# Second attention of a two-layer block: where half of V's product stands in TensorE's order, and where its copies stand in ScalarE's

## The reference

```
h = _ln(x, ln1_g, ln1_b) + shift                  # 256 features
qkv = (h @ Wqkv.T).reshape(b, n, 3, H, HD)        # H = 16, HD = 64
q = _ln(qkv[:, :, 0].transpose(0, 2, 1, 3), qn_g, qn_b)
k = _ln(qkv[:, :, 1].transpose(0, 2, 1, 3), kn_g, kn_b)
v = qkv[:, :, 2].transpose(0, 2, 1, 3)
scores = einsum('bhnd,bhmd->bhnm', q, k) / sqrt(HD)
attn = softmax(scores, axis=-1)
o = einsum('bhnm,bhmd->bhnd', attn, v)
x = x + o.transpose(0, 2, 1, 3).reshape(b, n, H * HD) @ Wout.T
gate = softmax(x.reshape(-1, d) @ Wgate.T, axis=-1)
```

## Time and profile before

| what | value |
|---|---|
| time before, median of 3 runs | 2434.58 us (2432.95 to 2436.35) |
| the profiled execution's own time | 2434.36 us |
| its span, first to last instruction | 2432.5 us |
| mean granted TensorE clock over the span | 0.970 |
| second attention, by the first and the last product that L1431 makes | 831.2 to 1929.9 us |
| TensorE busy over the span | 2318.0 us |
| VectorE, ScalarE, GpSimd busy | 1909.5, 1548.8, 1030.9 us |

### The profile page before, as it was taken

One profiled execution on the slowest core, in us unless ns is written; L12 is line 12 of the kernel. 1 busy time (PEld: TensorE's weight loads), 2 busy tenths in 40 slices (PEclk: granted clock), 3 DMA queues, 4 the chain that ended last, 5 costly groups with the idle time before them and its releaser, 6 DMA issues. The chain is left out here.

```text
span 2432.5 us, 67113 instructions
## 1 busy us (share of the span) xinstructions
PE 2318.0 (95%) x24912; PEld 2059.8 (85%) x24912; DVE 1909.5 (78%) x3776; ACT 1548.8 (64%) x2983; POOL 1030.9 (42%) x939
## 2 busy tenths in 40 slices
PE   7999999999999899999999999999999818999997
PEld 6888888899999788888888888888888717999996
DVE  8999999667667788888888888888888777666663
ACT  6999998766666456565656565656565554556653
POOL 5888888200000234343434343434343203445544
PEclk9999999999999899999999999999999856999998
DMA  4111110101001000000000000000000022334423
GB/s 146 43 41 41 43 39 25 53 25 32 28 26 33 27 17 15 16 14 17 13 17 13 17 13 17 13 17 13 17 13 17 15 61 71 91 95 87 97 52 35
DMA packets 78720, 89.21 MB, mean 37 GB/s; under 512 B 18480, under 2 KB 72496, under 8 KB 76080
## 3 DMA queue, kind: packets, MB, share of 16 engines
q1 hardware_dynamic: 66352, 71.10, 9.4%
q0 software_dynamic: 12288, 17.05, 4.3%
HBM read 62.42 MB, written 25.69 MB: 36 GB/s over the span
## 5 line engine op out<-in xcount | busy, mean ns | idle before, releaser
L1286 POOL TENSOR_TENSOR a_rq<-a_vq,minus_half 128x8 f32<-128x8 f32 x256 | 417.7, 1641 | 97.5 <-DVE a_vq L1310 97.5
L1230 ACT ACTIVATE a_sq<-a_bqk 128x512 f32<-128x512 f32 x256 | 152.9, 597 | 351.3 <-PE a_bqk L130 348.7
L1281 POOL TENSOR_TENSOR a_rstd<-a_veps,minus_half 128x1 f32<-128x1 f32 x63 | 34.8, 552 | 580.5 <-DVE a_veps L1357 580.5
L128 PE MATMUL a_bqk<-wqk_hi,a_h_lo 128*128 128x512 f32 x512 | 207.7, 406 | 3.5 <-DVE a_h_lo L1326 3.5
L130 PE MATMUL a_bqk<-wqk_hi,a_h_hi 128*128 128x512 f32 x512 | 201.2, 393 | 0.0
L129 PE MATMUL a_bqk<-wqk_lo,a_h_hi 128*128 128x512 f32 x512 | 201.0, 393 | 0.0
L1302 DVE TENSOR_TENSOR a_qk<-a_bqk,a_rq 128x512 f32<-128x512 f32 x256 | 175.9, 687 | 29.6 <-POOL a_rq L1286 29.5
L1956 ACT ACTIVATE e_u<-e_bu,e_b 128x512 f32<-128x512 f32 x128 | 88.3, 690 | 150.1 <-PE e_bu L130 147.7
L1215 ACT COPY a_vs<-a_ba 64x512 f32<-64x512 f32 x256 | 148.8, 581 | 53.5 <-PE a_ba L130 48.8
L2081 DVE TENSOR_TENSOR e_u_lo<-e_u,e_u_hi 128x512 fp32r<-128x512 f32 x128 | 88.4, 691 | 120.4 <-ACT e_u_hi L1961 120.3
L1294 DVE TENSOR_REDUCE a_ss<-a_sq 128x8 f32<-128x512 f32 x256 | 173.9, 679 | 2.6 <-ACT a_sq L1230 1.0
(11 more groups left out here) (334 smaller groups left out, 8036.6 us busy)
## 6 DMA issues: line engine op xcount, KB each, us to landing
a_qk<-gates_of_rows SPq DMA_DIRECT2D x32, 256.0 KB, 4.3
tokens<-a_xs SPq DMA_DIRECT2D x64, 128.0 KB, 1.7
out<-a_xs SPq DMA_DIRECT2D x64, 128.0 KB, 1.7
e_w<-in_fc1s SPq DMA_DIRECT2D x8, 1024.0 KB, 4.8
e_w<-in_fc2s SPq DMA_DIRECT2D x8, 1024.0 KB, 4.8
a_gate<-gates_of_rows SPq DMA_DIRECT2D x122, 64.0 KB, 2.5
X<-in_x SPq DMA_DIRECT2D x56, 128.0 KB, 2.1
wst<-in_qkv_w SPq DMA_DIRECT2D x16, 128.0 KB, 2.5
```

The costliest lines, as they stand in the source:

```text
L128: tensor.matmul(to, w_lo, x_hi, start=start, stop=False)
L1230: nc.scalar.activation(sq[:, n * BK:(n + 1) * BK], b_qk[:, n * BK:(n + 1) * BK], ACT.Square).then_inc(s["sq"], 1)
L1286: nc.gpsimd.tensor_tensor(rq[:, 8 * n:8 * n + 8], vq[:, 8 * n:8 * n + 8], g.mhalf[:, 0:8], ALU.pow).then_inc(s["rq"], 1)
```

## The change

In TensorE's turn `values(1)` moves from behind `values(0)` to behind the turns of the probabilities, where it stands between them and P V; in the turn that has no tile i-1 it stays. The first two groups of `turn_qk` move from in front of P V to behind it, so that all 16 turns of q and k stand between P V and the gate's product. The gate's product waits for the two copies of V's first half alone.

In ScalarE's turn `values_out(0)` moves from in front of the two PT copies to behind them, and `values_out(1)` from in front of the two `o_hi` to behind them. No instruction is added or taken away. (`values_out` gets a parameter that has its old value in each call.)

```diff
@@ scalar
-                if has(0):
-                    values_out(0)
                 if has(-1):
                     for n in range(2):
                         act.wait_ge(s[f"pT{n}"], i)
                         nc.scalar.copy(PT[:, 4 * n:4 * n + 4, :].rearrange("p j q -> p (j q)"), b_b[n][:, :])\
                             .then_inc(s["pT_out"], 1)
+                if has(0):
+                    values_out(0)
                 if has(-1) and not has(0):
...
-                if has(0):
-                    values_out(1)
                 if has(-1):
                     act.wait_ge(s["o"], i)
                     for n in range(2):
                         nc.scalar.copy(o_hi[:, n * BK:(n + 1) * BK], b_b[n][:, :]).then_inc(s["o_hi"], 1)
+                if has(0):
+                    values_out(1)
@@ tensor
                     values(0)
-                    values(1)
+                    if not has(-1):
+                        values(1)
...
                         last.then_inc(s[f"pT{n}"], 1)
-                if has(0):
-                    turn_qk(0, 2)
                 if has(-1):
+                    if has(0):
+                        values(1)
                     pe.wait_ge(s["pT_out"], 2 * i)
                     pe.sem_inc(s["pe_held"], 1)
...
                     last.then_inc(s["o"], 1)
                 if has(0):
-                    turn_qk(2, QG)
+                    turn_qk(0, QG)
                 if has(-2):
                     pe.wait_ge(s["xsT_out"], i - 1)
                     if has(0):
-                        pe.wait_ge(s["v_out"], 4 * (i + 1))
+                        pe.wait_ge(s["v_out"], 4 * i + 2)
```

More of the change, by code:

```diff
@@ L1210, in exps, with values_out @@
                     nc.scalar.activation(pr[:, :, :], pr[:, :, :], ACT.Exp, scale=SCALE1).then_inc(s["exped"], 1)
-                def values_out(n):
+                def values_out(n, halves=(0, 1)):
                     act.wait_ge(s["v"], 2 * i + n + 1)
-                    for b in range(2):
+                    for b in halves:
                         nc.scalar.copy(vs[n * S:(n + 1) * S, turn % 2, b, :],
```

## The result

| | before | changed |
|---|---|---|
| median of the runs | 2433.76 us (4 runs) | 2451.15 us (4 runs) |
| the profiled execution's own time | 2434.36 us | 2451.85 us |
| its span | 2432.5 us | 2450.0 us |

The ratio is 1.0074, with a 95% interval of 1.006 to 1.0087: 15 to 21 us lost. The prediction had 2433.8 us and a range up to 2440.

What follows compares the result with a forecast made beforehand. TensorE's in-order stream was taken as the bound; a 0.22 us wait for o was exchanged for 0.21 for kT. 0.01 us a turn over 61 turns, 0.6 us, came off 2434.36, giving 2433.8 us, range 2426.5 to 2440.

Steps and rivals of the forecast that it cites:

- The first wait goes: Between gate and projection, TensorE's wait for the first low part of o, 0.22 us a turn, was to disappear.
- P V 0.87 us earlier, the high parts with it: P V, with 8 turns fewer ahead, was to start at 1507.28; the high parts of o at 1508.50.
- the probabilities in time: Their turns on TensorE come 1.36 us earlier; the probabilities were to be ready with 0.16 us in hand.
- the PT copies in time: ScalarE's copies of the turned probabilities were to end 0.6 us ahead of P V's start.
- `kT` becomes the last to come: ScalarE's kT was to end at 1513.19, after TensorE could start the scores, making TensorE wait 0.21 us.
- TensorE's own time: When TensorE itself would reach the scores' load, without waiting for kT: forecast at 1513.04.
- Rival 1: ScalarE's join from V to qT overlaps, 0.52 instead of 0.61 us: 0.10 a turn faster, 2427.9 us; chance 0.18.
- rival 2: All three ScalarE joins with V overlap, TensorE bounds again: the whole 0.22 a turn kept, 2420.6 us; chance 0.06.
- the held step: TensorE's pe_held step, priced at 0.11 us from the gap before P V; taken as included in the scores' 0.06.
- The hand-off: Time from kT's end on ScalarE to the scores' first load on TensorE, forecast at 0.06 us.
- Rival 3: Between kT and scores, held step plus 0.13 give 0.24 us: 0.17 a turn slower, 2444.8; chance 0.16 with another rival.
- Nothing is added, so there are only places and waits: The prediction's premise for the whole change: only positions and waits were to alter, with no DMA moved.

Runs made afterwards that it cites:

- v_first_one_step: v_copies_first with the scores waiting for k_out alone: 2419.43 us, 0.9944 of the kernel before.
- k_out_one_step: The changed kernel with the scores waiting for k_out alone, the waits for q_out, v_out and lg_out dropped: 2437.97 us, 1.0022 of the kernel before.
- gate_count_alone: The kernel before with one edit: the gate's product waits for 4 i + 2 copies of V instead of 4 (i + 1): 2432.93 us, 0.9999.
- k_out_two_steps: The changed kernel with the scores' waits reordered to v_out, lg_out, q_out, k_out: 2444.91 us, 1.0046 of the kernel before.
- k_out_five_steps: The changed kernel with three more long-met waits (sq, v, v_out) behind that for k_out: 2460.91 us, 1.0113 of the kernel before.
- v_copies_first: The changed kernel with values_out(1) moved back ahead of the high parts of o: 2421.67 us, 0.995 of the kernel before.

## Why the prediction was wrong

*The first wait goes.* Right. In the changed kernel the gate's four loads and the projection's first follow each other at 0.11 us:

```profile
1872.00 0.53 PEld L1522 LDWEIGHTS a_ba<-wgate,a_xsT 128*128 128x128 f32 x4
1872.44 0.19 PEld L128 LDWEIGHTS a_bb<-w_parts,a_o_lo 128*128 128x128 f32 x1
```

The 0.22 us are gone; v_first_one_step keeps them (17.33 to 17.10 a turn, 14 us).

*P V 0.87 us earlier, the high parts with it, the probabilities in time, the PT copies in time.* Right, each within 0.04 us.

*`kT` becomes the last to come, and ends 0.15 us behind TensorE's own time.* Right, with 0.13 measured: it ended 5.91 us behind P V's load, and TensorE's own time was forecast at 5.78. First high part to the end of `kT` was 4.68 us against 4.69. The join from a copy of V to `qT` doesn't overlap (the pair ends at 1503.23, `qT` starts at 1503.25). ScalarE's timeline of the changed kernel:

```profile
1502.04 1.19 ACT L1215 COPY a_vs<-a_ba 64x512 f32<-64x512 f32 x2
1503.25 1.21 ACT L1266 ACTIVATE a_qT<-a_bqk,qn 128x1024 f32<-128x1024 f32 x1
```

Rival 1 and rival 2 fall with that row. The Trainium skill's sentence on ACTIVATEs that overlap by 93 ns ("ScalarE: Activation LUTs", "What ACT_TABLE_LOAD costs") doesn't hold at this join.

*"In the phase's first turn the scores' load came 0.06 us after `kT` ended, the held step included. So the scores load at 1513.25."* **This is the step that failed.** The hand-off was put at 0.06 us and measured 0.31 in the loop. The 0.06 was read rightly and belongs to another program: the first turn is written out, with one sequencer instruction at the late wait. The loop of the changed kernel has three. Rival 3 named the place and the sign and had 0.24 us, from the held step and the hand-off of P V; the runs show 0.31 from something else, and with one instruction in the loop, the held step within it, it is 0.11. Nor do the runs show that the held step has the price of 0.11 us that the prediction read off the gap ahead of P V: in the changed kernel the instruction that does it there starts at 1868.62, while a load of V's product still comes behind it, and P V loads at 1869.21.

The 0.05 us between 0.06 and 0.11 are not the loop against the written-out turn. In k_out_one_step the hand-off is 0.11 in a written-out turn too, with a constant count (third turn, ScalarE, then TensorE):

```profile
868.22 1.22 ACT L1270 ACTIVATE a_kT<-a_bqk,kn 128x1024 f32<-128x1024 f32 x1
```

```profile
869.55 1.25 PEld L1428 LDWEIGHTS a_ba<-a_kT,a_qT 64*64 64x64 f32 x64 [0.38 <-issue]
```

What differs is the instruction. Where one waits for `q_out` and `k_out` together, as in the first turn, it is already under way when `kT` ends. Those of the third and fourth turn of the changed kernel last 995 and 997 ns, and end 0.04 us after `kT` has ended (line 1426, from 860 to 900 us):

```profile
L1426 PEldq EVENT_SEMAPHORE  x2: 995/996/997, 871.5 to 889.0; - x2
```

Where it waits for `k_out` alone, or first, as in k_out_two_steps, it only starts 0.04 us after `kT` has ended.

*"Nothing is added, so there are only places and waits."* Wrong, and the root of it. The edit of the gate's count was costed at nothing because its wait was met 2 us early. It was; but the count had been shared with the scores. gate_count_alone shows that it costs nothing by itself, k_out_two_steps and k_out_one_step that it costs 0.1 us for each instruction once `kT` is late.

The 0.26 us by which a turn grew (17.33 to 17.59) are then: -0.22 for the wait that went, +0.13 because `kT` ends that much behind TensorE's own time for the scores, +0.31 for the hand-off, and +0.04 between scores and P V. The first two hang on TensorE's own time, which was never seen in this kernel: v_first_one_step has TensorE ready 5.75 us behind P V's load instead of the forecast 5.78, and with that they are -0.25 and +0.16. For the last, the scores' 64 loads take 1.05 us behind a wait and 1.02 without one. That is most of it, and no run was made on its cause.

k_out_one_step's median is also 2.4 us above what its 17.37 us turns explain (2433.18 + 61 x 0.04 = 2435.6). Its profiled execution took 2435.83 us, and its twelve runs lie between 2435.63 and 2443.59; I leave that open.

One slip in the sums changes nothing here: rivals 1 and 2 were taken from 2434.0 us, which already has the forecast's 0.6 us off, and rival 3 from 2434.36.

The range ended at 2440 because rival 3 got a price of 0.24 us and the small end of the chances. Its bound came from the nearest rows of the trace before, and in none of them did a wait for another semaphore stand behind the event that came last.

## What to carry to other kernels

In a loop, look at what the sequencer does between the event that comes last and the instruction that waits for it: put that wait last, have its neighbours' counts computed before, and leave out waits that another one implies. A count used in two places is computed once; changing one of them can put arithmetic behind a wait elsewhere. And when a wait is removed by moving an engine's work, ask which order of the other engine's queue leaves slack at both ends: here the copies of V fitted ahead of the high parts with 0.3 us to spare, and behind them they were late.

## What the runs showed that was not expected

A sequencer instruction of TensorE behind a wait that has just been met costs about 0.1 us, whether it multiplies, waits for something long met or both (hand-offs of 0.11, 0.22, 0.31 and 0.47 to 0.50 us for 1, 2, 3 and 5). Where the event comes half a us early, the same instructions cost nothing that can be measured (0.9999 in gate_count_alone).

A wait in which the late semaphore is the second of a pair handed on in 0.06 to 0.07 us, and one with it alone in 0.11, with a constant count as with a register's (k_out_one_step, 869.44 to 869.55 and 1495.49 to 1495.60). No run was made that changes the pairing alone, so this is read from traces. In k_out_five_steps the late wait is the second of a pair too (`sq`, `k_out`), which fits its hand-off being a little short of five times 0.1 us.

A copy of V's first half starts 0.12 us before the PT copies have ended (1483.66 against 1483.78 in v_copies_first), while one of the second half waits for its predecessor's end. So it is not the number of partitions alone that keeps such copies apart.
